# The second stage's P·V product with v stationary and the probabilities moving, two heads in the two column halves, and the division by the row sums behind it

## The reference

```python
h = shift_token(x)                       # half the channels come from the token before
q, k, v = split(h @ wqkv)                # 8 heads of 64
q, k = rotary_xpos(l2norm(q) * qs, l2norm(k) * ksc)
# windows of 128 queries; keys: own window and the one before, masked
attn = softmax(where(mask, -max, 8 * q @ k.T))
x = x + (attn @ v).reshape(b, n, 512) @ wo
h = (layernorm of shift_token(x)) * lg + lb
a, g = split(h @ w1 + b1)
x = x + (a * gelu(g)) @ w2 + b2
```

## Time and profile before

| | |
|---|---|
| median of three runs | 4847.38 us |
| span of the profiled execution | 4843.6 us |
| first stage, about | 0 to 1900 us |
| second stage, about | 1900 us to the end |
| share of the span: TensorE, its weight loads | 91%, 74% |
| VectorE, ScalarE, GpSimd | 71%, 53%, 56% |

### The profile page before, as it was taken

The page is one execution under the profiler, slowest core; times in us unless marked ns, Lnnn a source line. Parts: engine busy times, 40 slices in busy tenths (PEclk is TensorE's granted clock), DMA queues, the critical chain, the costliest instruction groups (busy, mean ns, idle before and its releaser), DMA issues.

```text
span 4843.6 us, 98674 instructions
## 1 busy us (share of the span) xinstructions
PE 4406.7 (91%) x36902; PEld 3602.1 (74%) x36992; DVE 3426.7 (71%) x5743; ACT 2548.9 (53%) x5920; POOL 2690.2 (56%) x1654
## 2 busy tenths in 40 slices
PE   5888888888888886999999999999999999999998
PEld 3666565666666654888888888888888888888887
DVE  3888888888888884666666666666666666666665
ACT  2433333333343323666666666666666666666664
POOL 4999999999999993333333333333333333333332
PEclk8999999999999997999999999999999999999999
DMA  4344333333343401000000000000000000000000
GB/s 77 52 57 55 52 45 46 49 45 46 45 57 50 57 12 54 11 17 15 15 20 13 15 20 13 15 20 24 15 25 20 19 26 17 22 20 24 21 19 25
DMA packets 128879, 151.18 MB, mean 31 GB/s; under 512 B 16959, under 2 KB 94614, under 8 KB 128406
## 3 DMA queue, kind: packets, MB, share of 16 engines
q1 hardware_dynamic: 128406, 144.63, 17.2%
HBM read 43.93 MB, written 25.17 MB: 14 GB/s over the span
## 4 chain that ended last, share of the span: by engine, by line
PE 38%; issue 9%; DVE 8%; ACT 3%; POOL 3%; SPq 0%; DMA 0%; DVEq 0%; POOLq 0%; ACTq 0%
PE b_X L1280 8%; PE b_M L1325 7%; PE b_F L1351 6%; PE b_M L1403 4%; PE b_F L1430 3%; PE b_S L1305 3%; PE b_S L1314 2%; ACT b_p L1039 2%; PE b_S L1296 1%; PE b_M L1394 1%; DVE b_hn L1138 1%; POOL b_rn L871 1%; PE b_X L1262 1%; DVE b_ss L1065 1%; DVE b_mx L1086 1%
## 5 line engine op out<-in xcount | busy, mean ns | idle before, releaser
L277 ACT ACTIVATE a_p<-a_S 128x512 f32<-128x512 f32 x1024 | 528.8, 602 | 1115.4 <-PE a_S L500 1115.4
L317 DVE TENSOR_REDUCE a_nm<-a_S 128x128 fp32r<-128x2048 f32 x256 | 584.8, 2285 | 181.6 <-PE a_S L459 178.3
L1039 ACT ACTIVATE b_p<-b_S,b_nb,b_rn 128x256 f32<-128x256 f32 (+1 forms) x1024 | 537.4, 534 | 223.4 <-DVE b_nb L1089 222.6
L1280 PE MATMUL b_X<-b_wqkv,b_hT 128*128 128x512 f32 x2304 | 650.8, 418 | 1.5 <-DVE b_hT L1113 1.3
L221 POOL TENSOR_TENSOR a_p<-a_p,a_zi 128x512 f32<-128x512 f32 x256 | 616.4, 2408 | 62.4 <-DVE a_zi L324 62.3
L213 POOL TENSOR_TENSOR a_z<-a_p 128x1024 f32<-128x1024 f32 x256 | 605.6, 2366 | 68.6 <-ACT a_p L277 68.6
L1351 PE MATMUL b_F<-b_hnT,b_w 128*114 128x256 f32 (+1 forms) x4608 | 628.1, 285 | 5.7 <-issue 5.7
L864 POOL TENSOR_TENSOR b_t<-b_t 128x512 f32<-128x512 f32 x128 | 165.7, 1295 | 823.5 <-DVE b_t L1063 823.5
L1351 PEld LDWEIGHTS b_F<-b_hnT,b_w 128*114 128x114 f32 (+1 forms) x4608 | 572.8, 177 | 19.4 <-issue 5.9
L327 DVE TENSOR_TENSOR a_p<-a_p,a_zi 128x1536 f32<-128x1536 f32 x256 | 541.8, 2116 | 8.8
L1098 DVE TENSOR_SCALAR b_a<-b_F,w_b 114x256 f32<-114x256 f32 (+1 forms) x384 | 183.8, 479 | 427.9 <-ACT b_g L960 427.9
(11 more groups left out here) (135 smaller groups left out, 8894.7 us busy)
## 6 DMA issues: line engine op xcount, KB each, us to landing
a_q<-a_parts SPq DMA_DIRECT2D x128, 256.0 KB, 9.9
a_k<-a_parts SPq DMA_DIRECT2D x128, 256.0 KB, 10.7
a_x<-in_x SPq DMA_DIRECT2D x16, 512.0 KB, 4.1
x_after_heads<-a_n SPq DMA_DIRECT2D x64, 128.0 KB, 1.7
b_x<-x_after_heads SPq DMA_DIRECT2D x16, 512.0 KB, 3.9
x_after_layer<-b_xo SPq DMA_DIRECT2D x32, 256.0 KB, 2.3
b_x<-x_after_layer SPq DMA_DIRECT2D x16, 512.0 KB, 3.9
b_x<-x_after_heads SPq DMA_DIRECT2D x32, 256.0 KB, 2.8
```

Of the source, the lines that this page charges most:

```text
L277: nc.scalar.activation(probs[u % NE][:, hs], S[:, hs], ACT.Exp, scale=HDIM ** -0.5).then_inc(s_exp, 1)
L317: nc.vector.tensor_reduce(out=negmax[u % 2][:], in_=S[:].rearrange("p h q -> p q h"), axis=AX.X, op=ALU.max, negate=True).then_inc(s_nm, 1)
L1039: last = nc.scalar.activation(probs[hf][:, i, keys(w_)], SB[:, i, keys(w_)], ACT.Exp, bias=nb[hf][:, i:i + 1], scale=rn[w_ % 2][:, h:h + 1 ...
L1280: last = nc.tensor.matmul(X[i][:], hT_of(k, a), wqkv[:, b, k, i * INNER:(i + 1) * INNER], start=(k == 0 and (a, b) == PART_PAIRS[0]), stop ...
```

## The change

The stationary operand of `times_v` becomes v (128 keys by 64 channels of one head) and the moving one `PT` (128 keys by 128 queries). `tile_position=(0, 64 * e)` puts the even head of a pair in columns 0 to 63 of the array and the odd one in columns 64 to 127, so that M collects channels by queries, already transposed; the loops put the two heads behind each other. The inverse row sums are now needed with queries along the free axis: VectorE inverts them at the start of the step (L1150's instruction, moved), GpSimd spreads them over 64 channels (`spread_inverses`, 128x512, into the half of `sq` that holds squares of k, at the start of its step), and TensorE transposes these instead of `o_n`, at the same place in its order. Since that overwrites M, ScalarE first copies M to `oU` (in the place of the copy to `oT`), and VectorE multiplies M by `oU` into `oT`, behind `low_hT` and ahead of `row_max(T, 0)`. `wo` waits for that product. Left out below: four waits on `s_c` that count one constant more.

```diff
@@ -625,6 +625,7 @@
     srow = [sb(f"srow{i}", [P, 4, LDIM]) for i in range(LAYERS)]
     mask = [sb(f"mask{i}", [P, 2, P], BF16) for i in range(2)]
     zero_col = sb("zero_col", [P, 1])
+    one_col = sb("one_col", [P, 1])
     carrier = sb("carrier", [P, 1])
     HIGH, LOW = 0, 1
     wqkv = sb("wqkv", [P, 2, CT, 3 * INNER], F32R)
@@ -646,8 +647,10 @@
     probs = [sb(f"p{i}", [P, 4, 2 * P]) for i in range(2)]
     rs = [sb(f"rs{i}", [P, LHEADS]) for i in range(2)]
     rinv = sb("rinv", [P, LHEADS])
+
+    rwide = sq[:, 1].rearrange("p h d -> p (h d)")
     PT = [sb(f"PT{i}", [P, 4, 2 * P]) for i in range(2)]
-    o_n = sb("o_n", [P, INNER])
+    oU = sb("oU", [P, IH, P])
     oT = sb("oT", [P, IH, P])
     hs = sb("hs", [P, TILES, P])
     stats = sb("stats", [P, 2, 6])
@@ -699,9 +702,10 @@
     s_PTe = sem("PT_evacuated")
     s_AV = sem("av")
     s_ri = sem("row_sums_inverted")
-    s_on = sem("o_normalised")
-    s_oT = sem("oT")
-    s_oTe = sem("oT_evacuated")
+    s_rw = sem("inverses_widened")
+    s_oU = sem("oU_evacuated")
+    s_R = sem("inverse_sums_spread")
+    s_oTn = sem("oT_normalised")
     s_wo = sem("o_projected")
     s_x2 = sem("x2")
     s_sh = [sem(f"shifted{i}") for i in range(TILES)]
@@ -870,13 +874,20 @@
             need(pool, s_pr, 2 * t - 2)
             nc.gpsimd.tensor_tensor(rn[p][:], ssc[:], half[:], ALU.pow).then_inc(s_rn, 1)
 
+        def spread_inverses(t):
+            pool.wait_ge(s_ri, t + 1)
+            need(pool, s_R, t)
+            nc.gpsimd.tensor_tensor(sq[:, 1], rinv[:].unsqueeze(2).to_broadcast([P, LHEADS, LDIM]),
+                                    one_col[:].unsqueeze(2).to_broadcast([P, LHEADS, LDIM]), ALU.mult).then_inc(s_rw, 1)
+
         nc.gpsimd.memset(zero_col[:], 0.0).then_inc(s_c, 1)
+        nc.gpsimd.memset(one_col[:], 1.0).then_inc(s_c, 1)
         for i in range(2):
             nc.gpsimd.memset(hT1[i][:].bitcast(F32), 0.0).then_inc(s_c, 1)
             nc.gpsimd.memset(a_sb[i][:], 1.0).then_inc(s_c, 1)
             nc.gpsimd.memset(mask[i][:], 0.0).then_inc(s_c, 1)
         nc.gpsimd.memset(hs[:], 0.0).then_inc(s_c, 1)
-        pool.wait_ge(s_c, 8)
+        pool.wait_ge(s_c, 9)
         for i in range(2):
 
             nc.gpsimd.affine_select(out=mask[i][:, i], in_=mask[i][:, i], compare_op=ALU.is_ge, fill=MASKED, base=0,
@@ -889,6 +900,8 @@
         def one(n, par, r, layer):
             for w_ in range(TILES):
                 T = TILES * n + w_
+                if tile_exists(T - 1):
+                    spread_inverses(T - 1)
                 if tile_exists(T - 2):
                     slot = (w_ - 2) % TILES
                     cols = slice(slot * P, (slot + 1) * P)
@@ -993,8 +1006,8 @@
                 if tile_exists(T + 1) or tile_exists(T - 2):
                     evacuate_hT(T, n, w_, layer)
                 if tile_exists(T - 1):
-                    act.wait_ge(s_oT, T)
-                    nc.scalar.activation(oT[:], M[:], ACT.Copy).then_inc(s_oTe, 1)
+                    act.wait_ge(s_AV, T)
+                    nc.scalar.activation(oU[:], M[:].rearrange("p (b q) -> p b q", q=P), ACT.Copy).then_inc(s_oU, 1)
                 if live:
                     exps(T, w_, 0)
                 if tile_exists(T + 1):
@@ -1130,6 +1143,10 @@
                 T = TILES * n + w_
                 p = w_ % 2
                 live, feed = tile_exists(T), seq_exists(n - 1)
+                if tile_exists(T - 1):
+                    dve.wait_ge(s_pr, 2 * T)
+                    need(dve, s_rw, T - 1)
+                    nc.vector.reciprocal(rinv[:], rs[1 - p][:]).then_inc(s_ri, 1)
                 if tile_exists(T - 2):
                     n2, w2_ = back(n, w_, 2)
                     p2 = par if w_ >= 2 else 1 - par
@@ -1145,16 +1162,12 @@
                     low_qkT(T, 1, p)
                 if feed:
                     value(T, 0, w_, layer)
-                if tile_exists(T - 1):
-                    dve.wait_ge(s_AV, T)
-                    nc.vector.reciprocal(rinv[:], rs[1 - p][:]).then_inc(s_ri, 1)
-                    dve.wait_ge(s_ri, T)
-                    nc.vector.tensor_tensor(o_n[:].rearrange("p (h d) -> p h d", d=LDIM),
-                                            M[:].rearrange("p (h d) -> p h d", d=LDIM),
-                                            rinv[:].unsqueeze(2).to_broadcast([P, LHEADS, LDIM]), ALU.mult
-                                            ).then_inc(s_on, 1)
                 if tile_exists(T + 1):
                     low_hT(T, w_)
+                if tile_exists(T - 1):
+                    dve.wait_ge(s_R, T)
+                    nc.vector.tensor_tensor(oT[:], M[:].rearrange("p (b q) -> p b q", q=P), oU[:], ALU.mult
+                                            ).then_inc(s_oTn, 1)
                 if live:
                     row_max(T, w_, 0)
                 if tile_exists(T - 1):
@@ -1317,14 +1330,16 @@
         def times_v(t, w_, hf):
             pe.wait_ge(s_PTe, 2 * t + hf + 1)
             slots = 1 if w_ == 0 else 2
-            for e in range(2):
-                for ps in range(2):
-                    i, h = 2 * e + ps, 4 * hf + 2 * ps + e
-                    for a in range(slots):
-                        first = hf == 0 and i == 0 and a == 0
-                        last = nc.tensor.matmul(M[:, h * LDIM:(h + 1) * LDIM], PT[hf][:, i, a * P:(a + 1) * P],
-                                                v[:, w_ if a == w_ % 2 else w_ - 1, h * LDIM:(h + 1) * LDIM], start=first,
-                                                stop=(hf == 1 and i == 3 and a == slots - 1), skip_group_check=True)
+            for ps in range(2):
+                b = 2 * hf + ps
+                for a in range(slots):
+                    for e in range(2):
+                        rows, h = slice(64 * e, 64 * e + 64), 2 * b + e
+                        last = nc.tensor.matmul(M[rows, b * P:(b + 1) * P],
+                                                v[:, w_ if a == w_ % 2 else w_ - 1, h * LDIM:(h + 1) * LDIM],
+                                                PT[hf][:, 2 * e + ps, a * P:(a + 1) * P],
+                                                start=(b == 0 and a == 0), stop=(b == IH - 1 and a == slots - 1),
+                                                tile_position=(0, 64 * e), skip_group_check=True)
             if hf == 1:
                 last.then_inc(s_AV, 1)
 
@@ -1389,15 +1404,16 @@
                 if live:
                     scores(T, w_, 0)
                 if tile_exists(T - 1):
-                    pe.wait_ge(s_on, T)
+                    pe.wait_ge(s_rw, T)
+                    pe.wait_ge(s_oU, T)
                     for b in range(IH):
-                        last = nc.tensor.transpose(M[:, b * P:(b + 1) * P], o_n[:, b * P:(b + 1) * P], ident[:])
-                    last.then_inc(s_oT, 1)
+                        last = nc.tensor.transpose(M[:, b * P:(b + 1) * P], rwide[:, b * P:(b + 1) * P], ident[:])
+                    last.then_inc(s_R, 1)
                 if tile_exists(T + 1):
                     projection_ready(T + 1, layer(0 if w_ < 3 else 1))
                     project(0, s_q)
                 if tile_exists(T - 1):
-                    pe.wait_ge(s_oTe, T)
+                    pe.wait_ge(s_oTn, T)
                     wo = W[layer(0 if w_ >= 1 else -1)]["o"]
                     for b in range(IH):
                         last = nc.tensor.matmul(M[:, 0:CH], oT[:, b], wo[:, b], start=(b == 0), stop=(b == IH - 1))
```

More of the change, by code:

```diff
@@ L974, in _ @@
         act.wait_ge(s_w, WEIGHTS)
-        act.wait_ge(s_c, 12)
+        act.wait_ge(s_c, 13)
         evacuate_hT(-1, -1, 3, lambda d: 0)
@@ L1114, in low_hT @@
                                     ).then_inc(s_hTl, 1)
-        dve.wait_ge(s_c, 12)
+        dve.wait_ge(s_c, 13)
         split_low(0)
@@ L1357, in _ @@
         pe.wait_ge(s_w, WEIGHTS)
-        pe.wait_ge(s_c, 12)
+        pe.wait_ge(s_c, 13)
         tile_parity["next"] = 0
```

## The result

The changed kernel takes 4879.47 us, median of four runs (4872.49 to 4883.20), beside 4848.99 of the kernel before (four runs, the three of above and one more): a ratio of 1.0061, 95% interval 1.0047 to 1.0075. It is slower by 30 us, where 38 us less were forecast. TensorE's work did shrink.

The account below looks back on a forecast made before the run. A chain through TensorE, ScalarE and VectorE was taken as the bound, TensorE waiting for `hn` every second tile. Gains and losses of four tiles summed to 1.19 us, times 32 is 38 us: 4809, own range 4790 to 4835, 80% range 4780 to 4905.

Parts of the forecast that it names:

- The matmuls: P·V records in two column halves overlap fully: 0.054 us each, 0.87 for 16, where 16 took 1.73.
- changes of shape: TensorE switching matmul shape around a P·V group: 0.20 us each, two a group, so 16 records take 1.27 us.
- without overlap: Rival: column halves do not overlap, 16 records take 1.73 us; 92 us lost, 4939; chance 0.15.
- with part of it: Rival: halves overlap in part, records 0.065 to 0.08 us, gain and new waits cancel; 4837; chance 0.13.
- with loads that wait: Rival: second half's loads wait for first half's matmuls, 0.162 us a record; 243 us lost, 5090; chance 0.03.
- the one in which TensorE alone counts: Rival: TensorE time saved counts in all 128 tiles, 0.91 us each; 117 us gained, 4731; chance 0.06.
- From c to F: Start of `hn` transposes (c) to transposes before `wo` (F): 0.46 us earlier in w_=3, 0.21 earlier w_=0, 0.42 later w_=1.
- from F to J: Transposes before `wo` (F) to probabilities' first transposes (J): row maximum 0.75 us late; w_=3 gains 0.13, w_=1 loses 0.60.
- From J to the next c, even tiles: Probabilities' transposes to next even tile's `hn` transposes: GpSimd's 1.28 us product delays `hn` to 3030.05, hidden before TensorE's 3030.08.
- From J to the next c, odd tiles: Probabilities' transposes to next odd tile's `hn` transposes: new product runs after L757, ends over 1 us before its reader, costs nothing.
- GpSimd's product holds `hn`: Rival: in even tiles a 2.78 us GpSimd product delays VectorE's `hn`; 53 us lost, 4900; chance 0.15.

Follow-up runs that it names:

- e1: The changed kernel with one wait more: GpSimd's product of inverse row sums also waits for VectorE's `hn` of that step; 4789.86 us, ratio 0.9875 to the kernel before.
- e10: The changed kernel with GpSimd's product waiting for `hn` only in even steps (w_ = 0 and 2); 4869.89 us, ratio 1.0054 to the kernel before.
- e2: The kernel before with only GpSimd's product and the earlier reciprocal added, the product's result not used; 4976.22 us, ratio 1.0254.

## Why the prediction was wrong

- **The matmuls**: right. A record is at 0.054, the full overlap. Too dear were only the two changes of shape, taken at 0.40 together: 0.15 comes once in the group and 0.11 behind it, so 16 records with both cost 1.02 + 0.11 = 1.13 us, forecast 1.27. The rivals without overlap, with part of it and with loads that wait are out, and so is the one in which TensorE alone counts: e1, without the hold, stays at 4790.
- **From c to F and from F to J**: right to 0.03 us in the tiles looked at, the wait for `oU` and the late row maximum included. But J before the change was read at the start of the load, and the matmul had stood 0.23 behind it (before, 3016.41 and 3060.23); a TensorE that waits starts both together (3022.57). So w_ = 3 gained 0.39 and not 0.13 by J and 0.80 and not 0.66 behind it, 1.19 against 1.16 measured from c to c. In w_ = 1 it is −0.35 and 0.80, 0.45 against 0.39 measured. These steps alone would have made the change better than forecast.
- **From J to the next c, even tiles**: the product did collide with `hn` and was just hidden, as worked out; e10 gives it 10 us at most, and the traces put this at the heads of the loop, which the prediction had not seen.
- **From J to the next c, odd tiles**: here it failed. The step said: "Behind gated GpSimd work the new product runs after L757 and beside reads from PSUM". It gave the product no price. But the earlier trace rows had shown that the second half of `hn` (L1140, 3007.39 to 3007.88) starts when L755 ends, and the row of L757 above shows that it isn't done until L757 is. One more instruction right behind L757 prolongs the same hold. Its end was compared with F, a reader 3 us away, and not with the instruction that it stood beside. The price is 1.0 us in two tiles of four: of the 88 us that the second stage of the changed kernel is longer than that of e1, 62 lie in the 64 steps that end in an odd tile.
- **The rival "GpSimd's product holds `hn`"** had the mechanism and the sign, but the wrong tiles and the wrong size: it took the product at 2.78 us, it took 1.04, and did its damage by its place in the queue. That its 4900 lies near the 4879 is luck, and so is that the 80% range, which reaches to 4905 mostly for its sake, holds the result.
- **Left out altogether**: that the granted clock can go down behind a longer wait of TensorE, and that a loop head makes VectorE late. The forecast counted each wait at its length. Of the 88 us between e1 and the changed kernel 18 lie in the 17 steps in which the clock fell behind a wait for `hn` (0.8 to 1.0 us each from w_ = 1 to 2, 1.4 from w_ = 3 to 0, outside the loop heads and the last group), and 6 in the nine loop heads, 0.7 each. In e1 TensorE doesn't wait for `hn` at the loop heads, and the clock falls behind no wait for it.

## What to carry to other kernels

When work is added to GpSimd's queue, look at what VectorE does from SBUF to SBUF at that time, for the whole run of GpSimd instructions that now stand without a gap, and let GpSimd wait for the VectorE instruction that the critical engine waits for. A wait added on an engine with slack can be worth nearly as much as work removed from the busiest one: 90 us in e1, where the lighter matmuls alone gave 109. A step of a plan that is priced at nothing needs its own row, with its end compared to everything beside it and not only to its reader.

## What the hardware showed that was not expected

FP32 products of 64 stationary and 128 moving columns, alternating between the two column halves, take 0.054 us a record (a group of 16 takes 1.02 us), against 0.109 in one half alone; with each half's products issued in a row a group takes 1.51. A stop of TensorE of 2.0 to 2.5 us between two busy stretches was followed by the 1.2 GHz level in 16 of 28 cases in the changed kernel (the scores 1.66 instead of 0.98 us), and in e2 one of 1.4 to 1.6 us in eight of 29. GpSimd's product of the eight inverse sums, each repeated 64 times, with a repeated constant took 1.04 us for 128x512, less than the 1.28 of one that reads full tiles (L868).
